# A three-layer decoder kernel: attention values in two groups, expert products 512 columns wide, biases as parts, GpSimd clearing, a new order table

## The reference, cut to what matters

```python
x = layernorm(x + causal_self_attention(x) @ W_proj + b_proj)              # layer 0
x = layernorm(x + cross_attention(x, ctx, mask) @ wo.T + bo)               # layer 1
# layer 2
attn_out = self_attention(x)                                               # no mask, no projection
gate     = softmax(x @ W_gate + b_gate)                                    # 8 experts
combine  = top-2 of gate, one-hot weighted                                 # (B, S, 8)
expert_out = einsum('bsd,edf->bsef', x, W_experts) + b_experts
moe_out  = einsum('bsef,bse->bsf', expert_out, combine)
x = layernorm(x + attn_out + moe_out)
```

## Time and profile before

| what | before |
|---|---|
| median of 3 runs | 1025.55 us (1025.3 to 1025.67) |
| profiled execution, its own time | 1025.35 us |
| its span, first to last instruction | 1023.6 us |
| TensorE busy / weight loads busy | 950.7 us (93%) / 817.3 us (80%) |
| VectorE / ScalarE / GpSimd busy | 763.3 / 537.1 / 396.6 us |

### The profile page before, as it was taken

One profiled execution on the slowest core, in us unless ns is written; L12 is line 12 of the kernel. 1 busy time (PEld: TensorE's weight loads), 2 busy tenths in 40 slices (PEclk: granted clock), 3 DMA queues, 4 the chain that ended last, 5 costly groups with the idle time before them and its releaser, 6 DMA issues.

```text
span 1023.6 us, 28458 instructions
## 1 busy us (share of the span) xinstructions
PE 950.7 (93%) x11008; PEld 817.3 (80%) x11008; DVE 763.3 (75%) x2092; ACT 537.1 (52%) x1083; POOL 396.6 (39%) x486
## 2 busy tenths in 40 slices
PE   2889888989999999999999999999999999999996
PEld 2677777878777777877778779999999999999985
DVE  7467667677766678677676678888888888888885
ACT  3456666757665566565665654444444444444422
POOL 2567767676756243352342522222222222222200
PEclk8899999999999999999999999999999999999999
DMA  4654554545444343343342422222222222222200
GB/s 145 164 143 125 138 146 123 151 124 157 117 114 123 99 126 105 85 126 95 96 114 75 125 64 64 64 75 79 75 73 64 78 75 75 63 77 78 73 28 22
DMA packets 98134, 100.85 MB, mean 99 GB/s; under 512 B 10696, under 2 KB 90576, under 8 KB 98000
## 3 DMA queue, kind: packets, MB, share of 16 engines
q1 hardware_dynamic: 98000, 99.03, 34.9%
HBM read 18.51 MB, written 4.19 MB: 22 GB/s over the span
## 4 chain that ended last, share of the span: by engine, by line
PE 61%; DVE 17%; POOL 14%; issue 5%; ACT 2%; DMA 0%; DVEq 0%; POOLq 0%; ACTq 0%
PE work L429 35%; PE work L547 6%; POOL probs L1004 6%; PE scores L526 6%; PE max_scores L502 5%; DVE neg_max L849 5%; DVE x_all L901 3%; PE work L556 2%; PE max_scores L505 2%; POOL k_parts L967 2%; POOL x_all L989 2%; PE scores L529 2%; POOL q_parts L967 2%; PE work L590 2%; DVE x_all L925 1%
## 5 line engine op out<-in xcount | busy, mean ns | idle before, releaser
L849 DVE TENSOR_REDUCE neg_max<-max_scores 128x4 f32<-128x512 f32 x384 | 256.8, 683 | 105.0 <-PE max_scores L505 86.3
L707 ACT ACTIVATE probs<-scores 128x512 f32<-128x512 f32 x384 | 226.6, 596 | 202.4 <-PE scores L526 158.2
L960 POOL TENSOR_TENSOR q_full<-q_full,q_parts 128x512 f32<-128x512 f32 x48 | 56.9, 1186 | 338.7 <-ACT q_parts L663 338.7
L526 PE MATMUL scores<-q_stack,k_stack 128*128 128x128 bf16 x1536 | 151.0, 221 | 2.0 <-DMA q_stack<-neg_max_t 1.1
L502 PE MATMUL max_scores<-k_stack,q_stack 126*128 126x128 bf16 x1536 | 150.1, 220 | 1.6 <-DVE neg_max L849 1.6
L547 PE MATMUL work<-probs,v_ones 128*32 128x128 f32 x3072 | 123.7, 279 | 23.8 <-POOL probs L1004 22.3
L429 PE MATMUL work<-w_hi,split_hi 128*128 128x256 f32 (+1 forms) x448 | 138.0, 308 | 1.0
L429 PE MATMUL work<-split_hi,w_hi 128*128 128x256 f32 x384 | 118.0, 307 | 19.5 <-DVE split_lo L758 19.5
L526 PEld LDWEIGHTS scores<-q_stack,k_stack 128*128 128x128 bf16 x1536 | 97.0, 98 | 44.5 <-issue 19.2
L925 DVE SCALAR_TENSOR_TENSOR x_all<-work,combine,x_all 128x256 f32<-128x256 f32 x256 | 110.8, 474 | 27.0 <-PE work L429 24.8
L502 PEld LDWEIGHTS max_scores<-k_stack,q_stack 126*128 126x128 bf16 x1536 | 104.8, 97 | 30.0 <-issue 8.9
(11 more groups left out here) (105 smaller groups left out, 2100.5 us busy)
## 6 DMA issues: line engine op xcount, KB each, us to landing
q_stack<-q_parts SPq DMA_DIRECT2D x288, 128.0 KB, 2.4
k_stack<-k_parts SPq DMA_DIRECT2D x288, 128.0 KB, 2.4
in_t<-in_xt SPq DMA_DIRECT2D x16, 256.0 KB, 2.9
x_all<-in_x SPq DMA_DIRECT2D x16, 256.0 KB, 2.9
in_t<-in_ct SPq DMA_DIRECT2D x16, 256.0 KB, 2.6
out<-x_all SPq DMA_DIRECT2D x16, 256.0 KB, 2.1
stage<-in_e SPq DMA_DIRECT2D x4, 512.0 KB, 5.2
stage<-in_qk SPq DMA_DIRECT2D x2, 512.0 KB, 4.0
```

Of the source, the lines that this page charges most:

```text
L526: mm = pe.matmul(dst[:, b, h2, :], head(KS, n, 2 * p + h2, b, rows), head(QS, n, 2 * p + h2, b, rows), start=(b + h2 == 0), stop=(b + h2 = ...
L707: act.activation(PR[g % PROBS][:, :, :, :], SS[g % 2][:, :, :, :], ACT.Exp).then_inc(probs_done, 1)
L849: dve.tensor_reduce(NM[n % 2][:, :, 2 * p:2 * p + 2], SM[g % 2][:, :, :, :], AX.X, ALU.max, negate=True).then_inc(max_read, 1)
L960: pool.tensor_tensor(FULL[x][:, :, :], FULL[x][:, :, :], PART[x][:, 0, :, :], ALU.subtract).then_inc(rest_done[x], 1)
```

## The change: what it does

1. `pv` is issued in two groups of four pairs (32 records each) instead of four groups of two, each waiting for the last of four exponentials (in layer 0, of four `causal` steps). The four buffers of probabilities and the two of `za` become one pool of six (`AT`), given out by the planned times.
2. An expert step is now one sequence of a pair of experts: 6 matmuls with 512 columns in place of 12 with 256. Its `combine` does two multiply-adds on the same rows of `x`, the second waiting for the first.
3. The experts' biases are cut into parts: 24 rows (high, low, high) against the combine weights (high, high, low), in two float32r matmuls with 256 columns. `gtop` gets three more small operations on VectorE and one more wait.
4. GpSimd clears the first two sets of stacks; the third is still cleared by VectorE, the ones as pairs in a 32-bit word, half as many elements as before.
5. TensorE starts with six products of GpSimd's ones (float32, 512 columns, 32 stationary columns) whose result is not used.
6. `TIMES` is replaced as a whole, with `PERIOD` 17.99 for layer 1 now 18.12.

```diff
-            for p in (2 * j, 2 * j + 1):
+            for p in range(4):
                     for b in range(PB):
                         for h2 in range(2):
...
+ATTN_BUFS = 6
+def assign_buffers():
...
+        if kind not in ("exp", "za"):
+            continue
+        j = min((i for i in range(ATTN_BUFS) if free_at[i] <= t), key=lambda i: free_at[i])
...
-            def expert(n, e):
-                if turn(n) == 1 and e % 2 == 0:
...
+            def expert(n, u):
+                g, b = divmod(u, PB)
...
+                mm = three_pass(mine("expert", n, u)[:, :],
+                                lambda c: hi[:, c, b * P:(b + 1) * P], lambda c: lo[:, c, b * P:(b + 1) * P],
+                                lambda c: wh[:, c, o:o + width], lambda c: wl[:, c, o:o + width])
...
-                    mm = pe.matmul(dst[:, b * D:(b + 1) * D], CBT[0:E, b * P:(b + 1) * P], EB[:, :], start=True, stop=True)
+                    mm = pe.matmul(dst[:, b * D:(b + 1) * D], CBT[0:BIAS_ROWS, b * P:(b + 1) * P], EBP[:, :],
+                                   start=True, stop=True)
...
-                dve.tensor_tensor(cb[:, :, 0:E], G1[:, :, :], G2[:, :, :], ALU.add).then_inc(combine_done, 1)
+                dve.tensor_tensor(cb[:, :, 0:E], G1[:, :, :], G2[:, :, :], ALU.add)
+                dve.tensor_tensor(cb[:, :, E:2 * E], G1[:, :, :], G2[:, :, :], ALU.add)
+                link(dve.tensor_tensor(CBH[:, :, :], G1[:, :, :], G2[:, :, :], ALU.add))
+                dve.tensor_tensor(cb[:, :, 2 * E:3 * E], cb[:, :, 0:E], CBH[:, :, :].bitcast(F32),
+                                  ALU.subtract).then_inc(combine_done, 1)
...
-                for b in range(PB):
-                    ins = dve.scalar_tensor_tensor(out=x[:, b, :], in0=src[:, b * D:(b + 1) * D],
+                for half in range(2):
+                    e = 2 * g + half
+                    ins = dve.scalar_tensor_tensor(out=x, in0=src[:, half * D:(half + 1) * D], scalar=CB[n % 2][:, b, e:e + 1],
+                                                   in1=x, op0=ALU.mult, op1=ALU.add)
+                    if half == 0:
+                        link(ins)
...
-            clear_stacks(0).then_inc(stacks_clear, 1)
             first_low(0)
             x_low(0, 0)
-            clear_stacks(1).then_inc(stacks_clear, 1)
...
-            clear_stacks(2).then_inc(stacks_clear, 1)
+            dve.memset(pairs_of(QS[2]), 0.0)
+            dve.memset(pairs_of(KS[2]), TWO_ONES).then_inc(last_stack_clear, 1)
...
+            for j in range(2):
+                pool.memset(pairs_of(QS[j]), 0.0)
+                pool.memset(pairs_of(KS[j]), TWO_ONES).then_inc(stacks_clear, 1)
...
+            pe.wait_ge(setup_p, 1)
+            for _ in range(6):
+                pe.matmul(WB[WORK_BANKS - 1][0:QUAD, :], VA[0][:, 0, 0:QUAD], VA[0][:, :, 0:2 * P], start=True, stop=True)
```

More of the change, by code:

```diff
@@ L30 @@
 MASKED = -(2.0 ** 100)
+TWO_ONES = 1.0019378662109375
 PAIRS = H // 2
 VG = D + E
+BIAS_ROWS = 3 * E
 VH = DH + 1
@@ L49 @@
 RB_COLS = 4 * D + VG
-PERIOD = [16.5, 17.99, 25.01]
+PERIOD = [16.5, 18.12, 25.01]
 TIMES = [
[4 rows of a table removed]
-     "max": [-16.18, -14.72, -13.26, -11.81, -10.35, -8.9, -7.45, -5.94], "nm": [-5.11], "maxt": [-4.53],
[4 rows of a table removed]
-     "norm": [31.53], "causal": [0.97, 2.38, 3.8, 5.21, 6.63, 8.04, 9.46, 10.88]},
[4 rows of a table removed]
-     "max": [-16.26, -14.84, -13.44, -12.01, -10.59, -9.18, -7.77, -6.3], "nm": [-5.95], "maxt": [-5.21],
[4 rows of a table removed]
-     "sum": [21.7], "rs": [22.7], "norm": [26.38]},
[4 rows of a table removed]
-     "max": [-24.67, -22.43, -20.19, -17.94, -15.7, -13.46, -11.22, -8.98], "nm": [-8.07], "maxt": [-7.07],
[3 rows of a table removed]
[L84 to L87, removed]
[4 rows of a table added]
+     "max": [-17.05, -14.11, -13.92, -12.14, -10.57, -9.19, -8.03, -5.23], "nm": [-4.18], "maxt": [-4.92],
[4 rows of a table added]
+     "norm": [31.87], "causal": [3.33, 3.78, 5.42, 5.59, 7.01, 9.0, 9.8, 10.41]},
[4 rows of a table added]
+     "max": [-16.49, -14.73, -13.66, -11.7, -11.09, -9.26, -8.48, -6.3], "nm": [-6.29], "maxt": [-4.73],
[4 rows of a table added]
+     "sum": [22.73], "rs": [23.72], "norm": [27.06]},
[4 rows of a table added]
+     "max": [-24.7, -22.53, -20.06, -18.06, -16.18, -14.04, -11.8, -9.77], "nm": [-9.01], "maxt": [-6.12],
[3 rows of a table added]
+     "gtop": [-18.27], "gateT": [-15.56], "cbt": [-15.57], "bias": [-14.62], "eb": [-14.19],
+     "expert": [-8.45, -5.48, -4.58, 1.1, 3.43, 6.17, 8.99, 12.86],
+     "combine": [-7.42, -4.45, -1.62, 1.41, 4.31, 7.38, 10.27, 13.67], "zadd": [12.79, 21.9], "stat": [24.92],
+     "rs": [31.89], "norm": [33.8], "store": [25.79]},
 ]
@@ L167 @@
 BANK, BANK_BEFORE = assign_banks()
+ATTN_BUFS = 6
+def assign_buffers():
+    slot, before = {}, {}
+    free_at, last = [-1e9] * ATTN_BUFS, [None] * ATTN_BUFS
+    for t, kind, n, part in ORDER:
+        if kind not in ("exp", "za"):
+            continue
+        j = min((i for i in range(ATTN_BUFS) if free_at[i] <= t), key=lambda i: free_at[i])
+        slot[(kind, n, part)], before[(kind, n, part)] = j, last[j]
+        free_at[j] = WHEN[("pv", n, part // 4) if kind == "exp" else ("zT", n, part)] + 0.01
+        last[j] = (kind, n, part)
+    return slot, before
+ATTN_SLOT, ATTN_BEFORE = assign_buffers()
 SPLIT_SLOTS = 3
@@ L180, in last_reader @@
 def last_reader(name, n):
-    if layer(n) == 2:
-        return "expert", n, E - 1
-    return ("q" if layer(n) == 1 and name == "x" else "v"), n, 0
+    pieces = {0: [("q", 0), ("k", 0), ("v", 0)], 1: [("q", 0)] if name == "x" else [("k", 0), ("v", 0)],
+              2: [("q", 0), ("k", 0), ("v", 1), ("expert", E - 1)]}[layer(n)]
+    kind, part = max(pieces, key=lambda piece: WHEN[(piece[0], n, piece[1])])
+    return kind, n, part
 SPLIT_BEFORE = {}
@@ L313, in bank_read, with attn, attn_free @@
             eng.wait_ge(done, n + 1 if once else turn(n) if reader == "ve" else count(reader, n, rpart))
+        def attn(kind, n, part):
+            return AT[ATTN_SLOT[(kind, n, part)]]
+        def attn_free(eng, kind, n, part):
+            use = ATTN_BEFORE[(kind, n, part)]
+            if use is None:
+                return
+            before, m, mpart = use
+            if before == "za":
+                eng.wait_ge(z_psum[mpart], m + 1)
+            else:
+                eng.wait_ge(pv_psum, PV_TURN[(m, mpart // 4)] + 1)
         def bank(kind, n, part=0):
@@ L323, in split_free @@
             kind, m, part = last_reader(*use)
-            done = {"expert": e_psum, "q": psum["q"], "v": v_psum[0]}[kind]
-            eng.wait_ge(done, count(kind, m, part) if kind == "expert" else m + 1)
+            done = {"expert": e_psum, "q": psum["q"], "k": psum["k"], "v": v_psum[part % PB]}[kind]
+            eng.wait_ge(done, count(kind, m, part) if kind == "expert" else turn(m) if kind == "v" and part else m + 1)
         def pair(n):
@@ L334, in decoder, with pairs_of @@
                     "e2": (WH0, WL0, 0, 2 * D), "e3": (WH0, WL0, 2 * D, 2 * D)}
-        def expert_weights(e):
-            hi, lo, o, _ = piece_to[f"e{e // 2}"]
-            return hi, lo, o + e % 2 * D
+        def pairs_of(stacks):
+            return stacks[:, :, :, :].rearrange("p h c t -> p (h c t)").bitcast(F32)
         FIRST = [s[:, :, :, :].rearrange("p h c t -> p (h c t)").bitcast(F32)[:, 0:C * 2 * D].rearrange("p (c n) -> p c n", c=C)
@@ L346, in decoder @@
         CONSTS = 5
-        S2_PIECE = {j: piece for piece, j in S2_TURN.items()}
         block = stack.enter_context(nc.Block())
@@ L375, in stack_rows @@
                 if n < STACKS and k == 0:
[L376 removed]
+                    if n == STACKS - 1:
+                        sp.wait_ge(last_stack_clear, 1)
+                    else:
+                        sp.wait_ge(stacks_clear, n + 1)
                 if n >= STACKS and k == 0:
@@ L444, in source, with source_ready @@
                 return SH[s], SL[s]
+            def source_ready(n):
+                if layer(n) == 1:
+                    pe.wait_ge(cl_done, turn(n))
+                else:
+                    pe.wait_ge(xl_done, n + 1)
             def feature_major(x, n, hi, lo):
@@ L465, in k @@
             def k(n, part):
-                if layer(n) == 1:
-                    pe.wait_ge(cl_done, turn(n))
+                source_ready(n)
                 feature_major("k", n, *source(n))
@@ L555, in z_tokens @@
                 for p in range(4):
-                    mm = pe.transpose(dst[:, p * P:(p + 1) * P], ZA[f][:, p, :], IDF)
+                    mm = pe.transpose(dst[:, p * P:(p + 1) * P], attn("za", n, f)[:, p, :], IDF)
                 mm.then_inc(z_psum[f], 1)
@@ L1055 @@
         "vg2": weight(w2[:, 2 * D:], a(L0_ffn_W_gate)),
-        "eb": a(L0_ffn_b_experts), "rows": rows, "cols": cols, "consts": consts,
+        "eb": np.tile(a(L0_ffn_b_experts), (3, 1)), "rows": rows, "cols": cols, "consts": consts,
     }
```

87 lines of the change are left out of this document (43 added, 44 removed), and 46 rows, old and new, of the table TIMES.

## The result

| | us, median (lowest to highest) | ratio to before, 95% interval |
|---|---|---|
| before | 1025.61 (1025.3 to 1026.11) | |
| after | 1009.31 (1008.56 to 1012.55) | 0.9847 [0.9825, 0.9868] |

A forecast was written before the change was run, and what follows sets the result against it. Items bound the run: TensorE in layer 2, TensorE plus one order stall in layers 0 and 1. Savings 24 + 13 + 20 + 5 = 62 us from 1025.35 give 963.4, median 963.6; range 932 to 1003.

The forecast's parts named there:

- TensorE's sum in layer 2: Layer 2: TensorE's need falls from 25.74 to 24.08 us an item, less 0.56 (experts), 0.7 (biases), 0.4 (pv).
- 512 columns: Layer 2 experts: 512-column products 0.225 us apart, six taking 1.35 against 1.42 for twelve; 0.56 us an item saved.
- rival D: 512-column float32r products no faster, merged pv saves nothing: 28 us less gain, 992 us; 0.24 together with B.
- The bias step: Layer 2: two float32r products take 0.35 us instead of 1.06, saving 0.7 us an item (0.4 to 0.8).
- Merged `pv`: All layers: two groups instead of four save 0.2 us for each of two merges, 0.4 an item (0 to 0.6).
- Layer 2, the step that failed: VectorE at 22.9 of 24.08 us; 0.4 given back for a stall in gtop; item 24.5, saving 20 us in all.
- Rival B: VectorE binds layer 2 (25.4 an item), new stall in layers 0 and 1: 989 us; 0.24 together with D.
- Layer 1: Moving norm- leaves about half the 0.86 us wait; item 18.45 to 17.65, saving 13 us (bounds 17.1 and 18.4).
- Rival C: Layer 1: row of maxima waits behind k's low parts in SyncE's queue; slower, 1036 us; chance 0.07.
- the ring: Rival C's layer 1 dependency loop, s20 through exp7, km, kl, ks2 and landing: 16.8 us, 0.3 under TensorE's 17.1.
- Layer 0: Walk of the new order: 1.42 us pv hole gone; item 17.3 to 15.8, saving 24 us.
- Start: Fewer VectorE clearings bring item 0's stacks earlier: 5 us saved (2 to 8); idle products give back what they cost.

The follow-up runs named there:

- the kernel with all meetings moved: Changed kernel with five added GpSimd waits on VectorE operations, the last in layers 1 and 2, whole computation kept: 956.61 us, 0.9321.
- the pair of kernels at 962.65 and 962.72: Changed kernel with five GpSimd waits, the fifth in layer 2 only: 962.65 us; the same with 256-column expert products and independent multiply-adds: 962.72 us.
- the kernel with narrow experts: Changed kernel with the five waits, expert products 256 columns wide and multiply-adds independent as before: 962.72 us, 0.9393.
- the kernel with one meeting left: Changed kernel with the first four added GpSimd waits, whole computation kept: 974.73 us, 0.9502; layer 2 item 24.43.
- the three kernels with a part undone: Changed kernel, no added waits, with narrow experts and independent multiply-adds: 986.18 us; with old float32 biases: 998.33; with multiply-adds unlinked, half the experts missing: 985.05.
- The old table: All changed code with the TIMES table of the kernel before, pv groups at the old second and fourth times: 1027.97 us, 1.0024.
- the two start experiments: Changed kernel without the six idle products: 1014.81 us, 0.987; changed kernel with the stack clearings given back to VectorE: 1011.76 us, 0.9857.

## Why the prediction was wrong

*What bounds the kernel:* right. Items times 16 gave the run, and the limits were named per layer.

*TensorE's sum in layer 2:* right in total (24.08; 24.05 measured, 23.73 without gaps), but by luck, not in its terms. 512 columns: I took 0.225 us apart. In the kernel with all meetings moved:

```profile
802.47 0.39 PE L473 MATMUL work<-w_lo,split_hi 128*128 128x512 f32 x1
...
802.70 0.39 PE L473 MATMUL work<-w_hi,split_lo 128*128 128x512 f32 x1
...
804.17 0.28 PE L473 MATMUL work<-split_hi,w_lo 128*128 128x256 f32 x1
...
804.28 0.28 PE L473 MATMUL work<-split_hi,w_hi 128*128 128x256 f32 x1
```

The wide ones start 0.233 apart (three in 0.70), the narrow ones 0.117: the pace per column is the same, as rival D had it, and the pair of kernels at 962.65 and 962.72 shows it in time. My 0.107 of columns plus a fixed 0.013 was wrong, and the 0.56 an item that hung on it wasn't there. The bias step took 0.43 for 1.06, near my 0.35. Merged `pv`: 1.01 to 1.08 for a group of 32 records against 2 x 0.57, so about 0.1 a merge, not 0.2. These make 0.8 to 0.9 of the 2.0 us between 25.74 and 23.73. Most of the rest I had at nothing: float32r products take 0.9 us an item less from start to start (17.1 before, 16.2 with all meetings moved), and just as little in the kernel with narrow experts, which has the same 132 products as before. The new order enters a row of float32r products 8 times an item instead of 10, each time at 0.20 to the next start instead of 0.12, and two longer distances inside such rows, 0.36 and 0.22, are gone; the first was a wait for VectorE's low part (777.05 in before). They left no gap in TensorE's busy time, because the record of a product, 0.28 long, covers them.

*Layer 2, the step that failed:* "In the walk `qr` meets `gtop` again. I give back 0.4 and take 24.5 for the item." TensorE's idle time in the item, put at 0.4, measured 2.2, and the item 26.25. The shape was right: VectorE's chain from `z1` to `nm` arrives just when TensorE wants it, and anything more goes into the item. Its size was not. I priced the meetings with GpSimd from the one that the kernel before showed in `gtop`, and walked the new order with bare durations; the runs show three, 2.84 us. By an estimate, 26.25 - 2.84 = 23.4 is the chain without them, below TensorE's 23.73, and so 2.5 us of the 2.84 reach the item. That estimate holds for the kernel with one meeting left, 23.4 + 0.86 = 24.3 against 24.43, and is 0.3 to 0.7 too low for the three kernels with a part undone. VectorE's own 22.9 was also wrong, on the other side: it needs 21.1, half of the difference because the 21.5 of before had a meeting of 0.96 in it (L842: 1.52 an item for 0.57). The serial multiply-adds cost what I took: 0.99 a pair against 0.87.

The Trainium skill (SBUF — State Buffer, Who interferes with whom) says that VectorE and GpSimd share a port pair as an exclusive lock, taken by VectorE operations with two SBUF inputs and by casts and `tensor_scalar` in their two-port modes, and never by `tensor_reduce`. The traces agree line by line: L896 and L960 are `tensor_scalar`, L916 a cast, L902, L917 and L998 have two SBUF inputs, while the reductions L908 (682 ns mean over 384, none above 693) show no such jump. I had named the rule for the new operations of `gtop` alone; it held for six lines in layers 1 and 2, and I should have laid each of them against each of GpSimd's in the new order.

*Rival B* had this mechanism, with 25.4 for layer 2: also too small. Below 25.74 it still was a gain; in fact the change costs layer 2 time.

*A second cost of the same holes,* in no case of mine: the clock. In after it fell to the 1.2 GHz level four times in layer 2 before the last item, each time for some 3.4 us, and these items take 1.1 to 1.4 us more. That isn't the clock's cost alone: a fall also shifts the meetings (L998 is down to 0.58 in these items, and one of the two operations before `maxt` takes 1.01 to 1.16). Before, TensorE had no gap in layer 2 and the level held. With all meetings moved it held too, up to the last item, and but for the first the items stay within 0.4 of 23.73. The old table, with items of 25.46, and the three kernels with a part undone have gaps of 0.7 to 1.0 us an item, and no fall between the first item and the last either; the two start experiments, with 1.7 to 2.2 us an item as in after, have ten and five. That goes with the gaps, but no run set gaps and changed nothing else.

*Layer 1:* "So about half of the 0.86 stays" failed. `norm` still met `kr`, and the two operations of `nm` met `kl` and `res`; the wait became 1.37 and ate the `pv` gain (0 instead of 0.8 an item). With the meetings moved layer 1 is at 17.4 in most items and at 17.6 on average, near my 17.65. Rival C: no wait for the row of maxima, the ring never closed.

*Layer 0:* the walk held. Most items take 15.7 to 15.8, the hole is gone, and the old table shows that the order did it. But six of the first and last take 16.3 to 18.6 (as some did before, up to 18.4), so 15 intervals gave 15.6 us, 1.04 each and not 1.5. The one of 18.6 holds a fall of the clock (at 256.5); in three runs without a fall there it takes 17.1.

*Start:* 4.2 up to the first `maxt`, near the forecast (5). The 4.8 to the second `maxt` are not the start's but the order's: with the old table this interval is still 17.07, and with the clearings back on VectorE it stays at 12.98. So 16 intervals of layer 0 gave 20 of the 24. The idle products were put at "gives back what they cost", and no gain or loss of theirs is to be seen.

So: start 4 for 5, layer 0 20 for 24, layer 1 2 for 13, layer 2 -14 for +20.

## What to carry to other kernels

When an order is changed, write down for both VectorE and GpSimd when each operation runs, and lay every small VectorE operation (with two SBUF inputs, or a cast or scalar form) over every GpSimd one: a 0.17 us operation took 1.04 us in nine items of nine. A line whose mean is far above its shortest is the sign, and a semaphore wait on the engine with slack removes it, here 53 us for five waits. Look again afterwards: the first four had made a new meeting. While such meetings exist, undoing a part of a change measures where the meetings fall, not the part.

## What the runs showed of the hardware that I had not expected

- float32r products start 0.46 ns a column apart at full clock in all three widths here: 0.117 us for 256, 0.122 for 264, 0.233 for 512; bf16 products of 512 columns take 0.22.
- The starts of the records don't tell who is held up. L896 started at 840.65, 0.07 before GpSimd's operation, and still took 1.27, while GpSimd's took 1.17, as long as its others of that size in the item (1.16). In layer 0 it also goes the other way. Here VectorE's operation, started 0.05 earlier, took its 1.22, and GpSimd's took 2.18; in nine later items GpSimd's low part of k takes 1.60 beside VectorE's L815, itself at 1.13 for 0.69:

```profile
84.77 1.22 DVE L849 TENSOR_TENSOR w_lo<-stage,w_hi 128x1024 fp32r<-128x1024 f32 x1
84.82 2.18 POOL L1032 TENSOR_TENSOR q_parts<-q_full,q_parts 128x512 bf16<-128x512 f32 x1 [0.89 <-ACT q_parts L726]
```

- GpSimd clears 2048 words per partition in 1.80 us, where VectorE takes 1.76, and its clearing at 5.31 to 7.11 left VectorE's L806 beside it (two SBUF inputs, at 5.54) at 1.23 us, against 1.21 and 1.23 for the same with GpSimd idle (13.89 and 5.43 in the run with VectorE's clearings): the clearing, which only writes, didn't hold it up.
